# Position lookups of a graph kernel moved from the first dense node stage into two edge stages, and that stage's turned rows copied by ScalarE

## The reference

```python
def gatv2_conv(x, src, dst, Wl, Wr, att, bias):
    xl, xr = (x @ Wl).reshape(n, H, D), (x @ Wr).reshape(n, H, D)
    e = einsum('ehd,hd->eh', leaky_relu(xl[src] + xr[dst], 0.2), att)
    alpha = softmax of e over the edges with the same dst
    return segment_sum(alpha[:, :, None] * xl[src], dst).mean(axis=1) + bias

h = relu(layer_norm(gatv2_conv(x, s, d, Wl1, Wr1, att1, b1), g1, be1) + x)
return layer_norm(gatv2_conv(h, s, d, Wl2, Wr2, att2, b2), g2, be2) + h
```

## Time and profile before

| | us |
|---|---|
| three executions | 5120.53, 5121.84, 5128.67 |
| median | 5121.84 |
| profiled execution, span from its first to its last instruction | 4774.0 |
| what a run has beyond that span (5121.84 - 4774.0) | 347.8 |

### The profile page before, as it was taken

One profiled execution on the slowest core, in us unless ns is written; L12 is line 12 of the kernel. 1 busy time (PEld: TensorE's weight loads), 2 busy tenths in 40 slices (PEclk: granted clock), 3 DMA queues, 4 the chain that ended last, 5 costly groups with the idle time before them and its releaser, 6 DMA issues. The chain is left out here.

```text
span 4774.0 us, 66002 instructions
## 1 busy us (share of the span) xinstructions
PE 3299.5 (69%) x14192; PEld 1865.8 (39%) x14192; DVE 3285.4 (69%) x10437; ACT 2707.8 (57%) x7707; POOL 2893.4 (61%) x2835
## 2 busy tenths in 40 slices
PE   1534188544996679996897999948855649974332
PEld 1534133222664533432564343325532225543331
DVE  1322199775996868887786888869978868873332
ACT  1422299796777967775575777726657735530000
POOL 4777687687994567773787555325567600027776
PEclk9755599655998989998998999979978869985555
DMA  8433288797668956663996544459979956753331
GB/s 292 123 98 92 102 279 279 288 406 258 203 193 272 335 191 210 210 213 126 298 321 201 159 160 156 133 197 341 337 243 347 338 161 220 227 181 106 97 99 53
DMA packets 685509, 1019.82 MB, mean 214 GB/s; under 512 B 109779, under 2 KB 293748, under 8 KB 683248
## 3 DMA queue, kind: packets, MB, share of 16 engines
q1 hardware_dynamic: 617296, 877.29, 54.6%
q0 software_dynamic: 65856, 113.13, 8.9%
q10 hardware_dynamic: 2016, 25.69, 1.3%
HBM read 640.44 MB, written 381.14 MB: 214 GB/s over the span
## 5 line engine op out<-in xcount | busy, mean ns | idle before, releaser
L984 DVE TENSOR_TENSOR conv_logits_leaky<-conv_logits_z,conv_logits_sloped 128x512 f32<-128x512 f32 x784 | 520.3, 688 | 123.0 <-ACT conv_logits_sloped L918 104.3
L918 ACT ACTIVATE conv_logits_sloped<-conv_logits_z 128x512 f32<-128x512 f32 x784 | 462.7, 596 | 184.2 <-PE conv_logits_z L880 125.0
L1250 PE MATMUL conv_aggregate_part<-conv_aggregate_weighed,conv_wlc 128*128 128x512 f32 x784 | 363.9, 608 | 37.6 <-DVE conv_aggregate_weighed L1332 37.5
L880 PE MATMUL conv_logits_z<-conv_logits_hdT,conv_logits_wsum 128*128 128x512 f32 x784 | 368.2, 613 | 4.9 <-DVE conv_logits_leaky L984 2.9
L887 PE MATMUL conv_logits_z<-conv_diffT,conv_logits_wl 128*128 128x512 f32 x784 | 352.9, 593 | 0.0
L1499 PE MATMUL conv_nodes_o_ps<-conv_nodes_wmean,conv_nodes_hT 128*128 128x128 f32 x1568 | 226.9, 288 | 80.6 <-ACT conv_nodes_hT L1581 76.9
L1332 DVE TENSOR_TENSOR conv_aggregate_weighed<-conv_aggregate_alpha,conv_diffT 128x512 f32<-128x512 f32 x392 | 258.7, 719 | 11.7 <-DMA conv_aggregate_alpha<-ALPHA 11.7
L1499 PEld LDWEIGHTS conv_nodes_o_ps<-conv_nodes_wmean,conv_nodes_hT 128*128 128x128 f32 x1568 | 192.2, 193 | 181.8 <-issue 111.2
L1588 ACT ACTIVATE conv_nodes_squares<-conv_nodes_o_ps 128x128 f32<-128x128 f32 x784 | 204.6, 277 | 102.5 <-PE conv_nodes_o_ps L1499 102.5
L117 POOL DMA_INDIRECT AGG<-gine_edges_rows,idx x196 | 194.0, 990 | 102.4 <-issue 101.2
L111 POOL DMA_INDIRECT gat_logits_hs<-H,idx x196 | 214.9, 1096 | 59.8 <-issue 57.7
(11 more groups left out here) (298 smaller groups left out, 10126.0 us busy)
## 6 DMA issues: line engine op xcount, KB each, us to landing
conv_aggregate_alpha<-ALPHA SPq DMA_DIRECT2D x392, 256.0 KB, 5.1
HX<-gine_finish_hx SPq DMA_DIRECT2D x98, 512.0 KB, 11.7
AGG<-gine_edges_zero ACTq DMA_DIRECT2D x14, 1792.0 KB, 33.4
gine_mlp_x<-x SPq DMA_DIRECT2D x98, 256.0 KB
gine_mlp_agg<-AGG SPq DMA_DIRECT2D x98, 256.0 KB
YT<-gine_mlp_yT SPq DMA_DIRECT2D x98, 256.0 KB, 3.6
gine_finish_x<-x SPq DMA_DIRECT2D x98, 256.0 KB, 7.2
gine_finish_yT<-YT SPq DMA_DIRECT2D x98, 256.0 KB, 11.5
```

The source lines that it names most:

```text
L880: pe.matmul(z[h][:, :], wsum[:, h * D:(h + 1) * D], hdT[j % 3][:, :], start=True, stop=True).then_inc(z_done[0], 1)
L918: act.activation(sloped[(H * (2 * j + c) + h) % S][:, :], z[h][:, :], ACT.Copy, scale=SLOPE).then_inc(sloped_made[c], 1)
L984: dve.tensor_tensor(leaky[H * c + h][:, :], z[h][:, :], sloped[(H * (2 * j + c) + h) % S][:, :], ALU.max).then_inc(leaky_made[c], 1)
L1250: last = pe.matmul(part[n % 2][:, :], g.wlc[:, h * D:(h + 1) * D], weighed[n % 2][:, h, :], start=(h == 0), stop=(h == H - 1))
```

## The change

The lookups of columns 2 and 3 leave the first `conv_nodes`. Those of the last 15 edge tiles (30 lookups) are made in the first `conv_aggregate`, two more in every third turn. Those of the other 34 tiles (68 lookups) are made in the second `conv_logits`, which goes through the edge tiles from the last to the first: two lookups ahead of the gathers of `fetch(j)` for the tile that is fetched 15 turns later, and a small copy into `idx` behind them. The ring of `keepn` goes from four buffers to three, `idx` from 18 columns to 16. In the first `conv_nodes`, `copy_turned` goes from VectorE to ScalarE, ahead of `square`.

```diff
+EARLY = 15
+SEEN = EARLY + 1
 # conv_logits
-            hd, keepn, ... = ..., m.sbs("keepn", [P, TILE], n=4), ..., m.sems("keepn_in", 4)
+            hd, keepn, ... = ..., m.sbs("keepn", [P, TILE], n=3), ..., m.sems("keepn_in", 3)
+        if spread:
+            pos, seen, place_kept = m.sb("pos", [P, SEEN, SUB // 2, 16], I32), g.seen, m.sem("place_kept")
-                    past(sp, hdT_made, j - 3)
+                    past(sp, hdT_made, j - 2)
+                def look_up(j):
+                    for s in range(SUB // 2):
+                        gather(pool, pos[:, j % SEEN, s, :], g.POS[:, :], g.idx[:, tile(j), 2 + s:3 + s]).then_inc(seen[j % SEEN], 16)
+                def keep_place(j):
+                    wait_alone(pool, seen[j % SEEN], 32 * (j // SEEN + 1) - (32 if j % SEEN < EARLY else 0), own)
+                    pool.tensor_copy(g.idx[:, tile(j):tile(j) + 1, 14:16], pos[:, j % SEEN:j % SEEN + 1, :, 0]).then_inc(place_kept, 1)
                 def fetch(j):
                     if j >= R:
                         wait_alone(pool, turned_done, j - R + 1, own)
+                    if spread:
+                        if j >= EARLY:
+                            wait_alone(pool, place_kept, j + 1 - EARLY, own)
+                        if j + EARLY < N:
+                            look_up(j + EARLY)
                     for s in range(SUB):
...
+                    if spread and EARLY <= j + 1 < N:
+                        keep_place(j + 1)
 # conv_aggregate
                 def look_up(n):
                     for s in range(SUB // 2):
                         gather(pool, pos[:, n, s, :], g.POS[:, :], g.idx[:, n, s:s + 1]).then_inc(g.looked, 16)
+                    if n % 3 == 0 and n // 3 < EARLY:
+                        e = N - EARLY + n // 3
+                        for s in range(SUB // 2):
+                            gather(pool, pos[:, N + n // 3, s, :], g.POS[:, :], g.idx[:, e, 2 + s:3 + s]).then_inc(g.looked, 16)
...
-                    pool.tensor_copy(g.idx[:, :, 12:14], pos[:, :, :, 0]).then_inc(pos_copied, 1)
-                    pool.tensor_copy(g.idx[:, :, 14:16], g.idx[:, :, 16:18]).then_inc(pos_copied, 1)
+                    pool.tensor_copy(g.idx[:, :, 12:14], pos[:, 0:N, :, 0]).then_inc(pos_copied, 1)
+                    pool.tensor_copy(g.idx[:, N - EARLY:N, 14:16], pos[:, N:N + EARLY, :, 0]).then_inc(pos_copied, 1)
 # conv_nodes
                     make_base(n % NB, n // NB)
-                    if not final:
-                        e, s = n // 2, n % 2
-                        gather(pool, pos[:, e, s, :], g.POS[:, :], g.idx[:, e, 2 + s:3 + s]).then_inc(g.looked, 16)
-                if not final:
-                    wait_alone(pool, g.looked, 16 * g.NTN, own)
-                    pool.tensor_copy(g.idx[:, :, 16:18], pos[:, :, :, 0]).then_inc(pos_copied, 1)
-                    pool.wait_ge(pos_copied, 1)
-                def copy_turned(k, i):
-                    n = i * NB + k
-                    dve.wait_ge(turned_done, n + 1)
-                    past(dve, o_done, n - 1)
-                    dve.tensor_copy(hT[k % 2][:, :], turned[k % 2][:, :]).then_inc(hT_made, 1)
-                steps = ([] if final else [(0, copy_turned)]) + [(2, invert), (2, scale), (3, finish)]
+                steps = [(2, invert), (2, scale), (3, finish)]
-                steps = ([(0, preload), (0, copy_turned)] if final else []) + [(1, square), (1, root)] + ([] if final else [(4, relu)])
+                steps = ([(0, preload)] if final else []) + [(0, copy_turned), (1, square), (1, root)] + ([] if final else [(4, relu)])
```

More of the change, by code:

```diff
@@ L760, in conv_logits @@
         if spread:
-            hd, keepn, hd_in, keepn_in = m.sbs("hd", [P, SUB, D], n=4), m.sbs("keepn", [P, TILE], n=4), m.sems("hd_in", 4), m.sems("keepn_in", 4)
+            hd, keepn, hd_in, keepn_in = m.sbs("hd", [P, SUB, D], n=4), m.sbs("keepn", [P, TILE], n=3), m.sems("hd_in", 4), m.sems("keepn_in", 3)
         else:
@@ L795, in load @@
                     sp.dma_start(hd[j % 4][:, :, :], node_rows(g.H2, g.NTN + tile(j))).then_inc(hd_in[j % 4], 16)
-                    past(sp, hdT_made, j - 3)
-                    sp.dma_start(keepn[j % 4][:, :], edge_span(g.KEEPN, tile(j), P)).then_inc(keepn_in[j % 4], 16)
+                    past(sp, hdT_made, j - 2)
+                    sp.dma_start(keepn[j % 3][:, :], edge_span(g.KEEPN, tile(j), P)).then_inc(keepn_in[j % 3], 16)
                 def store_rows(j):
@@ L851, in fetch @@
                             gather(pool, hs[j % R][:, s, :], g.HX.rearrange("n t d -> (n t) d"), g.idx[:, j, 12 + s:13 + s]).then_inc(rows_in[j % R], 16)
+                    if spread and EARLY <= j + 1 < N:
+                        keep_place(j + 1)
                 sweep(N, [(1 - R, fetch)] + ([(2, add_mlp_row)] if spread else []))
+                if spread:
+                    wait_alone(pool, place_kept, N - EARLY, own)
             @block.tensor
@@ L963, in spread_dst @@
                 def spread_dst(j):
-                    dve.wait_ge(keepn_in[j % 4], 16 * (j // 4 + 1))
+                    dve.wait_ge(keepn_in[j % 3], 16 * (j // 3 + 1))
                     dve.wait_ge(hd_turned, j + 1)
@@ L968, in spread_dst @@
                     past(dve, hdT_made, j)
-                    dve.tensor_tensor_scan(hdT[j % 3][:, ::-1], keepn[j % 4][:, ::-1], hdT_ps[:, ::-1], hdT[(j - 1) % 3][:, 0:1],
+                    dve.tensor_tensor_scan(hdT[j % 3][:, ::-1], keepn[j % 3][:, ::-1], hdT_ps[:, ::-1], hdT[(j - 1) % 3][:, 0:1],
                                            ALU.mult, ALU.add).then_inc(hdT_made, 1)
@@ L1150, in conv_aggregate @@
         power, std, rstd = (m.sbs(n, [P, SUB], n=2) for n in ("power", "std", "rstd"))
-        pos = None if final else m.sb("pos", [P, N, SUB // 2, 16], I32)
+        pos = None if final else m.sb("pos", [P, N + EARLY, SUB // 2, 16], I32)
         T = 1 if final else 2
@@ L1230, in look_up @@
                         gather(pool, pos[:, n, s, :], g.POS[:, :], g.idx[:, n, s:s + 1]).then_inc(g.looked, 16)
+                    if n % 3 == 0 and n // 3 < EARLY:
+                        e = N - EARLY + n // 3
+                        for s in range(SUB // 2):
+                            gather(pool, pos[:, N + n // 3, s, :], g.POS[:, :], g.idx[:, e, 2 + s:3 + s]).then_inc(g.looked, 16)
                 sweep(N, [(0, await_weighed), (4, add_base), (0, make_base), (5, add_row) if final else (0, look_up)])
                 if not final:
-                    wait_alone(pool, g.looked, 16 * (g.NTN + 2 * N), own)
-                    pool.tensor_copy(g.idx[:, :, 12:14], pos[:, :, :, 0]).then_inc(pos_copied, 1)
-                    pool.tensor_copy(g.idx[:, :, 14:16], g.idx[:, :, 16:18]).then_inc(pos_copied, 1)
+                    wait_alone(pool, g.looked, 16 * 2 * (N + EARLY), own)
+                    pool.tensor_copy(g.idx[:, :, 12:14], pos[:, 0:N, :, 0]).then_inc(pos_copied, 1)
+                    pool.tensor_copy(g.idx[:, N - EARLY:N, 14:16], pos[:, N:N + EARLY, :, 0]).then_inc(pos_copied, 1)
                     pool.wait_ge(pos_copied, 2)
@@ L1390, in conv_nodes @@
         power, std, rstd = (m.sbs(n, [P, SUB]) for n in ("power", "std", "rstd"))
-        pos = None if final else m.sb("pos", [P, g.NTE, 2, 16], I32)
         if final:
```

5 lines of the change are left out of this document (2 added, 3 removed).

## The result

The change makes the kernel slower. The median of five executions is 5168.81 us (5164.19 to 5173.00), against 5122.42 (5120.53 to 5129.65) for the kernel before; the ratio is 1.0084, 95% interval 1.0073 to 1.0095. The profiled execution after spans 5169.6 us.

A forecast was written before the change was run, and what follows sets the result against it. Bounds: POOL and VectorE full in the first node stage, POOL's queue in the first aggregate, TensorE in the second logits. Terms -8 + 35 + 10 + 3 = +40 us gave 5162 us, range 5135 to 5185.

The forecast's parts named there:

- Node stage, -8: First node stage: projections go from 2.69 to TensorE's 2.58 us apart in the 71 late steps, -8 us.
- ScalarE's 2.4: First node stage: ScalarE's step with the copy, 2.4 us; if TensorE could follow it, the gain would be -25 us.
- Aggregate, +35: First aggregate: 14 extra lookup pairs exposed on POOL's full queue, 1.25 us a lookup, +35 us.
- lower bound of 20: First aggregate: +20 us if after each extra pair three tiles run at the fast cycle of 5.40 us.
- Second logits, +10 and +3: Second logits' start: load of node tile 4 late behind POOL's 16 first lookups, +10 us; TensorE's lowered clock afterwards, +3.
- The clock's +3: Second logits: the pause lowers TensorE's clock to 1.2 GHz for some 4 to 8 us of work, +3 us.
- The steady step: Second logits: POOL's steady step with the lookups takes 9.8 of 10.08 us, fits by 0.2, costs nothing.
- rival 3: Second logits: POOL becomes the bound, its step passing 10.08 us; +10 more, 5172 us; 12%.
- rivals 1 and 2: First: TensorE's pace covers the aggregate's new lookups, 5127 us, 10%. Second: each engine gives all it has, 5130, 8%.
- rival 4: First aggregate: all new lookups stretched to 1.79 us; +15, 5177 us; 8%.
- 348 us around the span: Whole run: 348 us of the median lie around the profiled span of 4774.0 us, untouched by the change.
- late load: Second logits: load of node tile 4 waits behind SyncE's store of X, which waits for POOL's addition; +10 us, once.

The follow-up runs named there:

- e1: Kernel before with one edit: the first node stage's turned rows copied by ScalarE, its 98 lookups staying on POOL; 4770.62 us, ratio 0.9990 to the kernel before.
- a1: The kernel after, unedited, timed again on a slower chip: 5189.06 us, ratio 1.0083 to the kernel before.
- e4: The change without its 30 lookups in the first aggregate (results stood in for by others): 5155.29 us, ratio 1.0022 to the kernel before.
- e0: The kernel before, unedited, profiled a second time, on the fast chip: 4777.06 us.
- b1: The kernel before, unedited, profiled again on one of the slower chips: 5129.04 us.
- e7: The change with no lookups in the second logits' first eight fetches, all 68 made later: 5153.84 us, ratio 1.0046 to the kernel before.
- a2: The kernel after, unedited, once more on a slower chip: 5175.27 us, ratio 1.0077 to the kernel before.
- e5: The change with SyncE issuing a node tile's load ahead of the two stores in the second logits: 5185.39 us, ratio 1.0077 to the kernel before.
- e6 again: Repeat on a slower chip: kernel before with the 98 lookups spread over both node stages and the copy on ScalarE; ratio 0.9994 to the kernel before.

## Why the prediction was right, and where it was not

*Node stage, -8: the mechanism right, the gain in the mean half.* 2.58 us instead of 2.69 in the late steps, both moves needed (e1). TensorE was the floor, not ScalarE's 2.4. But the gain is blurred by a thing that the prediction left out. In a1 TensorE works at half clock for over 30 us at the stage's start, in e4 hardly at all; the windows of the same stretch in both:

```profile
1283.00:1308.00 25.00, 25.00 (x75) 15.83 (x75) 9.51 (x30) 11.18 (x53) 5.54 (x5) 0.50 0.21 64
```

```profile
1283.00:1308.00 25.00, 25.00 (x135) 15.88 (x135) 17.69 (x57) 22.75 (x107) 11.22 (x9) 1.00 0.48 152
```

The eight profiles with the change's node stage have 0 (e4) to 6 (a1) full steps of 4.9 us, each 2.3 more than at full clock. Their lengths less 2.3 us for each such step all lie within 536.4 to 537.9 us, 9 to 11 below e0 and b1, which have none. (Those two have only some 10 early steps of 2.58 and some 85 late ones, 85 x 0.11 = 9, where the first profile had 71.) The slow steps give back 6 on the mean (2.6 x 2.3), which leaves 4. The first profile of the kernel before has 1, e1 has 3. Whether the copy on ScalarE makes them more frequent, so few profiles can't say.

*Aggregate, +35: right mechanism, too much by 6, and 9 of what was measured is a thing that it left out.* Within one chip the measured term is 26 (e7 against b1) to 37 (a2 against b1), and 29 by the means of all profiles (343.4, 343.4, 341.5, 341.5, 345.8 and 356.5 against 311.7 to 323.6); a2 is the longest because nearly all its cycles have the long form. The extra lookups took the 0.94 + 0.30 that was forecast (2697.42, 2698.67). By the rule of the Trainium skill ("SBUF — State Buffer", on the engine ports) they were not to be stretched, and here the trace agrees. What the prediction read from the same rule for a lookup under the weighings, the traces leave undecided, since the second regular lookup is sometimes stretched there and sometimes not. Three sizes were off. The pair of tile 3 is covered like that of tile 0 (the first addition comes 37.9 us after the stage's start before and after), so 13 are exposed and not 14. A long cycle is 8.03 - 5.79 = 2.24 longer, and the 26 between are 5.61 instead of 5.79, so 12 pairs cost 26.9 - 4.7 = 22: near the prediction's lower bound of 20, not its pick. Each pair does cost the 2.5 us forecast (cycles of 7.90 and 8.43 beside 5.43 and 5.95); what is less is that fewer of the regular lookups are stretched. And the 13th cycle, with POOL's standstill of 7.1 us, which nothing in this stage's profile of before announces, is 14.74 - 5.79 = 9 us longer. Of these 31 us the stage's end gives 4 back, which leaves 343.4 - 316.3 = 27 for this pair of profiles.

*Second logits, +10 and +3: of the right sign, but a third too small, and the step false on the chips measured.* The prediction had POOL's addition late by the length of 16 lookups, SyncE's load behind it, and VectorE behind the load. Neither SyncE's order (e5) nor POOL's addition set the end: POOL waited for ScalarE, which stood still until the burst was over. The burst's length counts in full, +20. The clock's +3 is no term of the change on these chips: the kernel before has the pause and the low clock too, as a window of b1 and one of after show behind the pause:

```profile
2883.00:2887.00 4.00, 3.04 (x10) 0.70 (x10) 3.12 (x7) 3.07 (x8) 0.00 (x0) 0.50 0.01 2
```

```profile
2923.00:2927.00 4.00, 4.00 (x6) 1.69 (x5) 3.75 (x12) 3.23 (x8) 2.31 (x5) 0.50 0.04 14
```

The steady step fits, as forecast, with 0.8 us to spare instead of 0.2; rival 3 is out, rivals 1 and 2 with the aggregate's steps, rival 4 with the 0.94 us.

*348 us around the span: false, and without effect,* since it stood in the sum as a constant. The error was to read as overhead what was another kind of execution, most likely another chip; the profile of before could not show ScalarE's standstill, which made the logits' term. The terms as measured, -4 + 29 + 20 = 45, stand against 46, 42 and 46.

*The total of +40 was near in part by luck.* Against the terms as measured the forecast is 4 too low in the node stages, 6 too high in the aggregate and 7 too low in the logits, and two causes that it didn't have, POOL's standstill (9) and ScalarE's (20), stand in the places of a price too high and of a late load.

## What to carry to other kernels

Where an engine's queue is full, each instruction moved onto it costs its whole length, and one taken off another full engine gives only the distance to the next floor: here 98 lookups cost 49 us in their new places and gave about 4 in the old, 10 at full clock. Don't lengthen a stage's first burst of indirect DMAs; on the slower chips the same 68 lookups behind that burst cost nothing that could be measured. And compare a profile's span with the timed runs: where they differ by more than a few us, the profile may be of another kind of execution, and its idle times with it.

## What the runs showed that was not expected

- The same kernel takes 4777 us on one chip and 5129 to 5147 on two others, with the first logits 528 or 670 us long. On the slower ones ScalarE slows down or stops at the second logits' start while POOL issues indirect DMAs back to back (an idle time of up to 20.40 us; it is back 2.5 to 6.5 us behind the burst's end in all profiles of these chips but e6 again). VectorE is late without a visible reason in some of them too (7.16 us ahead of one subtraction in a1). What couples them isn't in the profile, and whether the longer first logits have the same cause wasn't looked into.
- TensorE, busy for 25.00 of 25 us, stayed at 1.2 GHz for over 30 us in one profile and for less than one tile in another of the same stage, which makes the stage's length vary by 14 us.
- POOL stood still for 6.7 to 7.5 us between two lookups, in all six profiles with the lookups of the aggregate, each time ahead of the kernel's 1094th indirect DMA, and in none without them. That is also the same place of the program each time, the last extra pair, so count and place can't be told apart. Its cause is open; a standstill of 7.8 us stands in the last stage of a1 and e5.
